# Attention: score and row products in opposite halves of the array, softmax sums by way of DRAM

## The reference, cut to what matters

```python
q, k, v = (proj(Wq), proj(Wk), proj(Wv))          # [b, 16, 1024, 16]
att = jnp.einsum('bhqd,bhkd->bhqk', q, k) * scale
causal = jnp.tril(jnp.ones((T, T), dtype=bool))
att = jnp.where(causal[None, None], att, -jnp.inf)
att = jax.nn.softmax(att, axis=-1)
out = jnp.einsum('bhqk,bhkd->bhqd', att, v)
out = out.transpose(0, 2, 1, 3).reshape(B, T, C)
return jnp.einsum('btc,dc->btd', out, Wo)
```

## Time and profile before

| | us |
|---|---|
| three runs | 2408.28, 2411.98, 2419.59 |
| median | 2411.98 |
| profiled execution, own time | 2414.42 |
| its span (first to last instruction) | 2412.6 |
| first attention: row products before the turns | 57.9 to 89.5 |
| first attention: turns 0 to 7 | 89.5 to 432.8 |
| second attention: turns 0 to 7 | 1768.1 to 2111.8 |
| busy in the span: PE, VectorE, ScalarE, GpSimd | 2034.7, 1599.6, 856.7, 446.7 |

### The profile page before, as it was taken

One profiled execution on the slowest core, in us unless ns is written; L12 is line 12 of the kernel. 1 busy time (PEld: TensorE's weight loads), 2 busy tenths in 40 slices (PEclk: granted clock), 3 DMA queues, 4 the chain that ended last, 5 costly groups with the idle time before them and its releaser, 6 DMA issues. The chain is left out here.

```text
span 2412.6 us, 32196 instructions
## 1 busy us (share of the span) xinstructions
PE 2034.7 (84%) x11288; PEld 1386.3 (57%) x11288; DVE 1599.6 (66%) x3514; ACT 856.7 (36%) x1599; POOL 446.7 (19%) x324
## 2 busy tenths in 40 slices
PE   7899999699999989757766385646689999999998
PEld 4466665388888867334433242323356666469997
DVE  3677773254544355779999999995567777246775
ACT  2255554122223222431112111111335555435775
POOL 0011110423333030001001100110001010105775
PEclk9699999799999999878887698868879999989999
DMA  4111110211110010200000000000121211018886
GB/s 158 42 36 38 44 35 10 83 57 53 52 52 17 0 53 1 86 1 9 9 3 7 18 9 9 0 0 18 36 47 35 47 36 29 9 37 255 235 234 125
DMA packets 52448, 122.19 MB, mean 51 GB/s; under 512 B 14224, under 2 KB 25232, under 8 KB 49488
## 3 DMA queue, kind: packets, MB, share of 16 engines
q1 hardware_dynamic: 42704, 107.40, 14.9%
q0 software_dynamic: 8832, 12.16, 2.9%
q10 hardware_dynamic: 768, 0.79, 0.1%
HBM read 84.09 MB, written 10.52 MB: 39 GB/s over the span
## 5 line engine op out<-in xcount | busy, mean ns | idle before, releaser
L672 DVE CUSTOM_DVE_ANT_0 a_junk<-pair,a_mask 128x512 f32<-128x512 f32 (+3 forms) x768 | 394.2, 551 | 188.1 <-PE pair L519 184.5
L633 ACT ACTIVATE a_prob<-pair 128x512 f32<-128x512 f32 (+3 forms) x768 | 329.0, 496 | 306.5 <-PE pair L543 303.4
L543 PE MATMUL pair<-a_qx,a_kx 98*128 98x512 f32 (+3 forms) x768 | 266.0, 393 | 6.8 <-ACT a_prob L633 6.7
L519 PE MATMUL pair<-a_kx,a_qx 96*128 96x512 f32 (+3 forms) x768 | 246.2, 391 | 22.7 <-DMA a_qx<-a_comp 17.9
L475 POOL TENSOR_SCALAR_AFFINE_SELECT a_prob<-a_prob 128x512 f32<-128x512 f32 x128 | 81.2, 635 | 700.2 <-ACT a_prob L633 700.2
L903 DVE TENSOR_TENSOR m_h<-pair,m_g 128x512 f32<-128x512 f32 x96 | 66.3, 691 | 211.3 <-PE pair L726 210.2
L1285 PE MATMUL pair<-h_stream,r_w_kz 128*128 128x512 f32 x192 | 103.9, 695 | 118.5 <-DVE r_region L1691 113.3
L724 PE MATMUL pair<-m_x_hi,m_w_lo 128*128 128x512 f32 x448 | 178.1, 398 | 26.5 <-POOL m_w_lo L788 24.4
L519 PEld LDWEIGHTS pair<-a_kx,a_qx 96*128 96x128 f32 x768 | 150.6, 204 | 70.4 <-DVE a_mx_raw L672 28.2
L543 PEld LDWEIGHTS pair<-a_qx,a_kx 98*128 98x128 f32 x768 | 143.0, 193 | 74.4 <-ACT a_prob L633 39.3
L725 PE MATMUL pair<-m_x_hi,m_w_hi 128*128 128x512 f32 x448 | 176.8, 395 | 0.0
(11 more groups left out here) (305 smaller groups left out, 4254.7 us busy)
## 6 DMA issues: line engine op xcount, KB each, us to landing
mx_raw<-in_L_ffn_experts SPq DMA_DIRECT2D x69, 512.0 KB, 4.9
m_raw<-in_L_cond_experts SPq DMA_DIRECT2D x18, 1024.0 KB, 4.8
a_kx<-a_comp SPq DMA_DIRECT2D x96, 128.0 KB, 2.4
a_qx<-a_comp SPq DMA_DIRECT2D x360, 32.0 KB, 2.0
r_w_ring<-in_r_q_w SPq DMA_DIRECT2D x8, 512.0 KB, 3.9
m_raw<-in_L_cond_experts SPq DMA_DIRECT2D x6, 512.0 KB, 3.4
token_rows<-mx_h_rows SPq DMA_DIRECT2D x2, 1040.0 KB, 8.1
x_stream<-in_x SPq DMA_DIRECT2D x1, 2048.0 KB, 10.6
```

The costliest lines, as they stand in the source:

```text
L519: nc.tensor.matmul(first_bank[t % FR][:, 0:c1 - c0], qx[0:PRODUCT, m % 2, a, i * P:(i + 1) * P], kx[0:PRODUCT, m % 3, a // 2, c0:c1], star ...
L543: nc.tensor.matmul(score_bank[t % SR][:, q0:TT], kx[0:ROWS, n % 3, a // 2, j * P:(j + 1) * P], qx[0:ROWS, n % 2, a, h * TT + q0:(h + 1) * ...
L633: nc.scalar.activation(prob[:, i % RING, a, q0:TT], score_bank[t % SR][:, q0:TT], ACT.Exp, scale=SCALE).then_inc(s["b_exp"], 1)
L672: nc.vector.tensor_tensor_reduce(out=junk[:, t % 2, 0:cols], in0=first_bank[t % FR][:, 0:cols], in1=mask[:, m0:m0 + cols], scale=1.0, scal ...
```

## The change

* **Operands.** A head has 48 contraction rows (50 with the maxima), alone. Even heads lie in partitions 0 to 49, odd heads from 64 on; two heads share a tile (`rows_of`). `qx` has three buffers, as `kx`; no zeros are needed, and the ones rows are left by setting all of `kx` to 1 on GpSimd beforehand.
* **Order of products.** `FIRSTS_AFTER` goes. One row product follows each score product, and with the heads in the order 1, 0, 3, 2 it is always of the other half: score 0 (lower), row 1 (upper), score 1 (upper), row 0 (lower), and so on.
* **Values** of step i-1 move from the end of step i to behind its second product.
* **`comp`** gets two more copies of the high part (`twin`, one ScalarE operation of 128 x 1024 per half), so that one DMA places three parts: 4 DMAs for keys, 8 for queries, 2 per half for maxima.
* **Value projections** serve two groups at a time; there is one (16 matmul instructions) per turn instead of two.
* **ScalarE takes over** the copies of values and of maxima from VectorE. `maximum` writes to the PSUM bank that it reads; `junk` and its wait go.
* **Normalization** of all groups but the last: the value bank is copied to `o_all`, the sums go to DRAM, come back as 64 x 64, get a reciprocal (VectorE), go to DRAM, and come back broadcast over 32 partitions each into `factor`; then one VectorE product of 128 x 1024 per group. SP issues 7 DMAs for it. `sums` and `spread` stay for the last group only.
* One more barrier with clearing of semaphores (`end_layer`) between the recurrent layer and the last branch.

```diff
-PRODUCT = 3 * 2 * HD
+PRODUCT = 3 * HD
-FIRST = [(a, i, c_) for part in (range(4), range(4, QT)) for a in range(GH) for i in part for c_ in range(i // 4 + 1)]
+FIRST = [(a, i, c_) for part in (range(4), range(4, QT)) for i in part for c_ in range(i // 4 + 1) for a in (1, 0, 3, 2)]
-SMALL = (("max", 0, 1), ("sums", -1, 1), ("spread", -1, 1), ("qk", 2, 0), ("qk", 2, 1), ("max", 1, 0),
-         ("v", 1, 0), ("v", 1, 1), ("sums", 0, 0), None, None, ("spread", 0, 0))
+SMALL = (("max", 0, 1), None, None, ("qk", 2, 0), ("qk", 2, 1), ("max", 1, 0), ("v", 0, 0), None, None, None, None, None)
+NORM = {2: 0, 3: 1, 6: 2, 7: 3, 9: 4}
+NORM_LAST = {1: 0, 2: 1, 4: 2, 5: 3, 6: 4, 8: 5}
...
             order.append(("scores", n, i, a))
-            if (i, a) == (0, 1) and n:
-                order += [("values", n - 1, NS - 1), ("copy", n - 1, 1)]
-            for f in range(found, found if closing else min(NF, found + FIRSTS_AFTER[i][a])):
-                order.append(("first", m, f))
+            if (i, a) == (2, 0) and n > 1:
+                order.append(("norm", n - 2, 5))
+            if not closing:
+                order.append(("first", m, found))
...
+            if a == 1 and i:
+                order.append(("values", n, i - 1))
+            elif a == 1 and n:
+                order += [("values", n - 1, NS - 1), ("copy", n - 1, 1)]
...
-        if i:
-            order.append(("values", n, i - 1))
+        norm = (NORM_LAST if closing else NORM).get(i)
+        if n and norm is not None:
+            order.append(("norm", n - 1, norm))
...
+        def rows_of(a, n):
+            return slice(a % 2 * 64, a % 2 * 64 + n)
...
+                    for a in range(GH):
+                        rows = slice(64 + a * HD, 64 + a * HD + HD)
+                        sp.dma_start(kx[rows_of(a, PRODUCT), m % 3, a // 2, :].bitcast(F32), comp[rows, 0:3, :].bitcast(F32))\
+                            .then_inc(s["k_in"], 16)
...
+                def norm(n, step):
+                    group = slice(n * HALF, (n + 1) * HALF)
+                    if step == 0:
+                        sp.wait_ge(s["o_cp"], (n + 1) * HALF)
+                        sp.dma_start(totals[n, :, :], o_all[HD:P:SLOT, group, :].rearrange("p h t -> p (h t)"))\
+                            .then_inc(s["n_out"], 16)
+                    elif step == 1:
+                        sp.wait_ge(s["n_out"], (n + 1) * 16)
...
+                        sp.dma_start(total[:, :, :], totals[n, :, :].rearrange("a (p c) -> p a c", p=64)).then_inc(s["n_in"], 16)
+                    elif step == 3:
+                        sp.wait_ge(s["n_rcp"], n + 1)
+                        sp.dma_start(inverses[n, :, :].rearrange("a (p c) -> p a c", p=64), inverse[:, :, :])\
+                            .then_inc(s["n_back"], 16)
+                    elif step == 4:
+                        sp.wait_ge(s["n_back"], (n + 1) * 16)
...
+                        for a in range(GH):
+                            sp.dma_start(factor[a * SLOT:(a + 1) * SLOT, :], inverses[n, a:a + 1, :].broadcast_to([SLOT, T]))\
+                                .then_inc(s["n_wide"], 16)
...
-                    nc.tensor.matmul(first_bank[t % FR][:, 0:c1 - c0], qx[0:PRODUCT, m % 2, a, i * P:(i + 1) * P],
-                                     kx[0:PRODUCT, m % 3, a // 2, c0:c1], start=True, stop=True).then_inc(s["a_mm"], 1)
+                    r = rows_of(a, PRODUCT)
+                    nc.tensor.matmul(first_bank[t % FR][:, 0:c1 - c0], qx[r, m % 3, a // 2, i * P:(i + 1) * P],
+                                     kx[r, m % 3, a // 2, c0:c1], start=True, stop=True).then_inc(s["a_mm"], 1)
...
                     nc.scalar.activation(comp[:, 0, half(h)], bank_of("qk", m, h), ACT.Copy).then_inc(s["hi"], 1)
+                    act.wait_ge(s["hi"], m * HALF + h + 1)
+                    nc.scalar.activation(comp[:, 2:4, half(h)], comp[:, 0:1, half(h)].bitcast(F32).broadcast_to([P, 2, TT]), ACT.Copy)\
+                        .then_inc(s["twin"], 1)
+
+                def copy_values(pair, v):
+                    act.wait_ge(s["vp"], pair * 2 + v + 1)
...
+                def copy_maxima(m, h):
+                    act.wait_ge(s["t_mm"], m * HALF + h + 1)
...
                     nc.vector.tensor_tensor_reduce(
-                        out=junk[:, t % 2, 0:cols], in0=first_bank[t % FR][:, 0:cols], in1=mask[:, m0:m0 + cols],
+                        out=first_bank[t % FR][:, 0:cols], in0=first_bank[t % FR][:, 0:cols], in1=mask[:, m0:m0 + cols],
                         scale=1.0, scalar=-3.0e38, op0=ALU.add, op1=ALU.max,
...
+                    elif step == 5:
+                        dve.wait_ge(s["n_wide"], (n + 1) * GH * 16)
+                        tile = o_all[:, n * HALF:(n + 1) * HALF, :].rearrange("p h t -> p (h t)")
+                        nc.vector.tensor_tensor(tile, tile, factor[:, :], ALU.mult).then_inc(s["n_done"], 1)
```

More of the change, by code:

```diff
@@ L414, in place_keys @@
                     sp.wait_ge(s["used"], used("qk", m, 1))
-                    if m >= 3:
+                    sp.wait_ge(s["twin"], (m + 1) * HALF)
+                    if m < 3:
+                        sp.wait_ge(s["ones"], m + 1)
+                    else:
                         sp.wait_ge(s["b_exp"], (m - 2) * NS * GH)
-                    for p in range(PAIRS):
-                        rows = slice(64 + p * 32, 96 + p * 32)
-                        for part, low in enumerate((0, 1, 0)):
-                            sp.dma_start(kx[part * 32:part * 32 + 32, m % 3, p, :].bitcast(F32), comp[rows, low, :].bitcast(F32))\
-                                .then_inc(s["k_in"], 16)
+                    for a in range(GH):
+                        rows = slice(64 + a * HD, 64 + a * HD + HD)
+                        sp.dma_start(kx[rows_of(a, PRODUCT), m % 3, a // 2, :].bitcast(F32), comp[rows, 0:3, :].bitcast(F32))\
+                            .then_inc(s["k_in"], 16)
                 def place_queries(m, h):
@@ L455, in _ @@
                         place_maxima(*which)
+                    elif what == "norm":
+                        norm(*which)
                     elif what == "split" and which == [NG - 1, 1]:
@@ L496, in qk_projection, with v_projection @@
                     last.then_inc(s["proj"], 1)
-                def v_projection(m, v):
-                    bank = take("v", m, v)
+                def v_projection(pair, v):
+                    m = 2 * pair
+                    bank = take("v", pair, v)
                     for t in range(4):
@@ L526, in maxima @@
                     for i in range(4):
-                        last = nc.tensor.matmul(bank[0:2 * GH, i * P:(i + 1) * P], mx[:, 4 * h + i, :, :].rearrange("p a x -> p (a x)"),
+                        last = nc.tensor.matmul(bank[0:2 * GH, i * P:(i + 1) * P], mx[:, 4 * h + i, :, :, :].rearrange("p r x q -> p (r x q)"),
                                                 c.neg_ident[:, :], start=True, stop=True)
@@ L567, in sums @@
                     for i in range(TT // P):
-                        last = nc.tensor.matmul(bank[:, i * GH:(i + 1) * GH], o_raw[:, h, i * P:(i + 1) * P],
+                        last = nc.tensor.matmul(bank[:, i * GH:(i + 1) * GH], o_all[:, n * HALF + h, i * P:(i + 1) * P],
                                                 c.sum_pick[:, :], start=True, stop=True)
@@ L648, in _ @@
             def _(dve):
-                for a in range(GH):
-                    nc.vector.memset(qx[:, 0, a, :].bitcast(F32), 0.0).then_inc(s["zero0"], 1)
                 dve.wait_ge(s["mask"], 16)
@@ L713, in add_result @@
                                                    op0=ALU.add, op1=ALU.add).then_inc(s["used"], 1)
-                does = {"qk_use": lower, "v_use": copy_values, "first": maximum, "split": split_maxima, "max_use": copy_maxima,
-                        "sums_use": reciprocals, "spread_use": divide, "out_use": add_result}
+                does = {"qk_use": lower, "first": maximum, "split": split_maxima,
+                        "sums_use": reciprocals, "spread_use": divide, "out_use": add_result, "norm": norm}
                 for what, *which in ORDER:
@@ L2594, in _constants @@
     pick = (extra[:, None] & (row[:, None] // SLOT == np.arange(GH)[None, :])).astype(f)
[L2595 to L2596 removed]
+    causal = np.zeros((P, TT + P), f)
+    causal[:, TT:] = np.where(row[None, :] > row[:, None], -1.0e30, 0.0)
     freq = np.arange(D)
```

167 lines of the change are left out of this document (85 added, 82 removed).

## The result

Four runs of the changed kernel took 2471.82 to 2474.88 us, median 2474.45; before, on the same chip, 2411.39 (2408.28 to 2419.59). The ratio is 1.0254, 95% interval 1.0227 to 1.0280: **slower by 2.5%**. The forecast was 2351, the range ended at 2415.

The account below looks back on a forecast made before the run. A loop through exponentials, values and next product bounds a turn: 31.7 us plus 7.8 small work, taken as 38.5. Gains of 62 us for both attentions, barrier 1.1, from 2414.4, median 2.4 lower: 2351 us; 8-in-10 range 2275 to 2415.

Parts of the forecast that it names:

- PE's work with overlap: In a turn: products in opposite halves overlap fully, 21.0 us become 10.5, PE's work 24.9 us; 35.3 without overlap.
- The other engines' work: In a turn: VectorE goes from 29.6 to 27.0 us, ScalarE from 22.3 to 26.3.
- The loop of 31.7 us: In a turn's twelve steps: exponentials, values and the next product wait for each other, 31.7 us whatever the halves do.
- the small work on top: In a turn: projections, `twin`, copies and VectorE's excess over the loop add 7.8 us to it.
- The twelve steps: Loop time of each step in a turn: 2.7, 3.1, 2.6, 2.1, 2.7, 4 x 2.65, 3.1, 2.6, 2.1 us.
- the 38.5 taken and the 39.5 summed: Length of a turn: loop and small work sum to 39.5 us; 38.5 taken because banks smooth a part.
- Its steps 3, 4 and 6: Steps of a turn ending in projections, which starve ScalarE for about 1 us each; small work adds 2.8, 1.9 and 1.6.
- rival D: In the turns: PE's waits lower its clock; 2432 us if low half the time; chance 0.14, including a longer loop.
- the copy of the value bank: In a turn: ScalarE's copy of this bank adds 0.5 us to the small work.
- VectorE's norm product: In a turn: the new 128 x 1024 product takes VectorE 1.22 us.
- The rest of the change: In a turn: one v projection fewer saves PE 1.85 us, sums and spread 3.9; the DRAM normalization costs 0.
- Rows alone and turn 0: Ahead of the turns: row products alone, 31.6 us, gain 3; the first turn falls from 48.2 to 38.5 + 4.7, gain 5.

Follow-up runs that it names:

- e13: Kernel before, with score and row products contracted over 64 of the 96 and 98 partitions; 2450.84 us, ratio 1.0172.
- e1: Kernel before, with values of a step moved behind the second score product of the next step; 2462.76 us, ratio 1.0199.
- e10: Changed kernel, value bank copy moved to (4, 2), norm product to step 5, two unused 128-row products added per diagonal step; 2378.66 us.
- e6: Kernel before, with row products contracted over 48 and score products over 50 rows; 2580.19 us, ratio 1.0717.
- e8: Changed kernel, value bank copy moved from (5, 0) to (4, 2), VectorE's norm product from step 2 to step 5; 2439.75 us.
- e7: Changed kernel plus two unused products of 128 rows and 512 columns in each diagonal step; 2457.25 us, ratio 1.0188.
- e5: Changed kernel without row halves, their order, `twin` and ScalarE's maxima copies (full 96 and 98 rows, late values); 2367.85 us, ratio 0.9820.
- e4: Changed kernel with heads 0 and 1 in the lower half, 2 and 3 in the upper; 2652.84 us, ratio 1.0971.

## Why the prediction was wrong

* **PE's work with overlap: right.** Pairs start together, and a pair costs what one full product cost (242 against 236 ns). Missing was the change of mode behind projections and maxima, 1.1 us a turn in e13; the changed kernel has one v projection and no sums, so some 0.9 us by the same differences, an estimate.
* **The other engines' work.** VectorE was put at 27.0 us a turn and is busy for 29.7, ScalarE at 26.3 and is busy for 26.1. No run shows VectorE as the bound of these turns.
* **The loop of 31.7 us and the small work on top: borne out in the main.** (The twelve steps as listed add up to 31.6.) e1 shows that early values cost 4 us a turn, and e10, where the clock is 1.00, has 40.1 us a turn against the 38.5 taken and the 39.5 summed. Its steps 3, 4 and 6 are 4.86, 4.68 and 4.34 against 4.9, 4.6 and 4.25. Steps 7 and 8, without either, are 2.29 and 2.56 against 2.65. The remainder lies mostly in steps 0, 10 and 11, three of the eight that also carry the added products.
* **The step that failed: "Against it: PE works for two thirds of each step, and no wait is much over 1.5 us".** With this rival D, the clock, was set at 0.14 with the loop's excess in it, and the turns were priced at full clock. It treated the granted clock as a matter of PE's waits, since the windows ahead of turn 0 had both the earlier trace rows. e6 shows the clock at 0.80 with no wait at all. In the changed kernel the products are of 48 and 50 rows and their time is halved by the overlap as well. That the clock's loss here is the rows' doing is carried over from e6 and not shown by itself. Its price is the 61 us from e8 to e10, net of the added products. Rival D's own estimate, 2432 for a clock low in half of the time, was nearest; with PEclk at 0.82 the clock was low in a third.
* **Missed: two waits that take the place of removed ones, 35 us by e8.** The prediction put 0.5 us a turn on the copy of the value bank, which delays the values by 2.3; and it cost VectorE's norm product as 1.2 us of VectorE alone, where it also holds GpSimd's cut from 0.64 to 1.54 us, in the loop.
* **The sum.** From 2351: the loop 1.6 us longer a turn, 14 turns, and a rest of some 5 us give e10's 2379; the clock 61; the two waits 35: 2475. The steps are the differences between runs, so that they must add up; taken in another order, clock and waits would share the 96 us otherwise (the added products alone gave 17 in e7, the moves alone 35 in e8).
* **The rest of the change was priced a little high.** Fewer v projections, no sums and spread and the DRAM round trip were put at 5.75 us less PE a turn (35.3 against 41.1), nothing waiting for DRAM. e5 has 37.0, 4.1 less, and PE is busy for 98% of it.
* **Rows alone and turn 0:** 34.1 us and a clock of 0.60, where 28.6 was forecast. Alternation of halves doesn't help where VectorE sets the pace, and the clock there was no better.

What stays open: how much of the low clock in the changed kernel is the rows' and how much PE's idle time (e6 has 0.80 with none, e4 0.62 with 8% and less full-row work); at which row count between 64 and 50 the turns lose their full clock; how e6's result divides between the number of rows and the zeros among them (in the kernel before, half of a product's query rows are zeros, and the first 48 keep that share on average); and the price of the added products inside e10, so that 61 us is the clock's cost only net of them.

## What to carry to other kernels

An edit that makes TensorE do the same sums with fewer rows can lower its clock, as 48 and 50 rows did here: read the granted clock of the stretch, and try the edit's row count alone in the old order before building on the gain. Price an order by the loop through all engines (product, exponential, cut, values), each queue included, since what stood behind a product may now stand in front of one. Where a change has several parts, run it without its boldest one: here that is the kernel to keep.

## What the runs showed of the hardware

* TensorE's granted clock in turns 1 to 5 with PE busy throughout and the same instructions in the same order: 1.00 with 96 and 98 rows, 1.00 with 66 and with 64, 0.80 with 48 and 50.
* Full-row products that nobody needs raised it from 0.79 to 1.00, and the kernel became 61 us faster for them.
* Two products in opposite row halves: starts 3 to 4 ns apart, 242 ns from pair to pair of 512 columns, 338 where other work stood before the first. Single full-row products: 236, and 337 behind values.
* Products of 64 rows behind full-row work start 0.15 to 0.2 us later than products of 66 (542 against 345 ns behind a v projection).
* GpSimd's 128 x 512 cut beside a VectorE product from SBUF and SBUF: 1.54 us instead of 0.63, and its end is 0.49 us behind the product's, wherever in the product it began.
* Row maximum of 512 columns written to PSUM: one every 0.65 us, not 0.61; the accumulator's read 0.14 us, not 0.08.
